# Attention in 64-row halves of TensorE's array: three score banks, untransposed outputs, and the products with the values issued once per two steps of 128 keys

## What is computed

```python
scores = jnp.einsum('bqhd,bkhd->bhqk', q, k) * scale      # 16 heads of 16 features, scale 0.25
probs = jax.nn.softmax(scores, axis=-1)                   # over 1024 keys
out = jnp.einsum('bhqk,bkhd->bqhd', probs, v).reshape(B, S, H)
return out @ wo.T
```

## Time and profile before

| what | us |
|---|---|
| median of 3 runs | 3612.48 |
| the profiled execution | 3616.42 |
| its span | 3614.8 |
| TensorE matmul busy | 3226.5 (89%) |
| TensorE weight load busy | 2116.2 (59%) |
| VectorE busy | 2386.9 (66%) |
| ScalarE busy | 1894.9 (52%) |
| GpSimd busy | 584.8 (16%) |

### The profile page before, as it was taken

The page is one execution under the profiler, slowest core; times in us unless marked ns, Lnnn a source line. Parts: engine busy times, 40 slices in busy tenths (PEclk is TensorE's granted clock), DMA queues, the critical chain, the costliest instruction groups (busy, mean ns, idle before and its releaser), DMA issues. The chain is left out here.

```text
span 3614.8 us, 64942 instructions
## 1 busy us (share of the span) xinstructions
PE 3226.5 (89%) x19056; PEld 2116.2 (59%) x19057; DVE 2386.9 (66%) x4072; ACT 1894.9 (52%) x3374; POOL 584.8 (16%) x846
## 2 busy tenths in 40 slices
PE   5888888849999999999999999997956999999980
PEld 4766666634545455454554545544845888888870
DVE  5666666648888878878878878862567444444436
ACT  3555555513676666666666666664523333333320
POOL 1222222210000000000000000000123444444430
PEclk7899989968999999999999999998878999999995
DMA  1333333321111111111111111114932111111119
GB/s 33 105 104 104 104 104 104 109 99 52 41 54 45 49 51 43 54 41 53 46 48 53 41 54 43 51 31 141 289 105 81 47 51 51 49 49 51 49 46 367
DMA packets 195841, 279.74 MB, mean 77 GB/s; under 512 B 26792, under 2 KB 129472, under 8 KB 195792
## 3 DMA queue, kind: packets, MB, share of 16 engines
q1 hardware_dynamic: 154320, 209.90, 17.9%
q0 software_dynamic: 16128, 44.06, 3.9%
q10 hardware_dynamic: 25344, 25.17, 2.2%
HBM read 158.37 MB, written 118.49 MB: 77 GB/s over the span
## 5 line engine op out<-in xcount | busy, mean ns | idle before, releaser
L779 DVE TENSOR_REDUCE b_mxq<-b_p_m 128x1 f32<-128x1024 f32 x1024 | 1205.5, 1219 | 312.7 <-PE b_p_m L833 304.6
L737 ACT ACTIVATE b_probs<-b_p_e 128x512 f32<-128x512 f32 x2048 | 1112.0, 595 | 509.6 <-PE b_p_e L887 504.8
L887 PE MATMUL b_p_e<-b_qst,b_kst 128*128 128x512 f32 x2048 | 799.7, 436 | 5.9 <-ACT b_probs L737 5.9
L887 PEld LDWEIGHTS b_p_e<-b_qst,b_kst 128*128 128x128 f32 x2048 | 343.5, 187 | 599.6 <-ACT b_probs L737 577.2
L833 PE MATMUL b_p_m<-b_kst,b_qst 128*128 128x512 f32 x2048 | 645.3, 402 | 29.9 <-DMA b_vst<-v_d 24.5
L862 PE MATMUL b_p_o<-b_probs,b_vst 128*32 128x512 f32 x4104 | 546.5, 605 | 0.9 <-ACT b_probs L737 0.9
L833 PEld LDWEIGHTS b_p_m<-b_kst,b_qst 128*128 128x128 f32 x2048 | 388.0, 191 | 116.6 <-issue 24.9
L1443 ACT ACTIVATE d_act<-d_p_up 128x512 f32<-128x512 f32 x136 | 81.3, 597 | 487.3 <-PE d_p_up L1505 487.3
L753 POOL DMA_DIRECT2D o_d<-b_o_s x64 | 34.8, 544 | 1637.9 <-DVE b_o_s L805 1637.9
L1520 PE MATMUL d_p_y<-w2T,d_hT 128*128 x1096 | 258.7, 379 | 0.8 <-ACT d_hT L1437 0.8
L1505 PE MATMUL d_p_up<-up_hi,d_xh 128*128 x544 | 250.7, 461 | 1.5 <-DVE d_xl L1462 1.5
(11 more groups left out here) (259 smaller groups left out, 4160.5 us busy)
## 6 DMA issues: line engine op xcount, KB each, us to landing
b_qst<-qk_d SPq DMA_DIRECT2D x384, 64.0 KB
b_kst<-qk_d SPq DMA_DIRECT2D x384, 64.0 KB
x1y_d<-a_x1y SPq DMA_DIRECT2D x32, 512.0 KB, 3.9
qk_d<-a_hi SPq DMA_DIRECT2D x32, 512.0 KB, 2.8
qk_d<-a_lo SPq DMA_DIRECT2D x32, 512.0 KB, 3.7
v_d<-a_v_s SPq DMA_DIRECT2D x16, 1024.0 KB, 6.9
b_vst<-v_d SPq DMA_DIRECT2D x64, 256.0 KB
c_xy<-x1y_d SPq DMA_DIRECT2D x16, 1024.0 KB
```

What stands on the lines that cost most here:

```text
L737: nc.scalar.activation(probs[e // 2 % 4][:, (e % 2) * 512:(e % 2 + 1) * 512], p_e[e % 2][:], ACT.Exp, scale=SCALE).then_inc(s["e_done"], 1)
L779: V_.reduce_max(mxq[half][:, j:j + 1], p_m[j % 2][:], AX.X).then_inc(s["m_red"], 1)
L887: mm(p_e[a][:], kst[r][h][:, kt * P:(kt + 1) * P], qst[r][:, a * 512:(a + 1) * 512], start=True, stop=True).then_inc(s["e_ps"], 1)
```

## The change

Attention: `kst` has one tile per pair, with head 0 on partitions 0 to 63 and head 1 on 64 to 127, and every score and maximum matmul uses the 64 rows of its head. Queue order on TensorE is now score e, maximum product 4kt + e, for e = 0 to 3, where `column(j)` puts the maximum products of scores of head 0 to head 1 and the other way round. There are three score banks. The values of two steps (16 instructions instead of 8) are issued once per two steps, behind score 2 and maximum product 2 of the even steps. `probs` has eight buffers instead of four. GpSimd splits the maxima before their transpose, which goes into a score bank (slot `NEG_AT + 1`); ScalarE negates. The output is no longer transposed or divided: ScalarE copies `p_o` and GpSimd stores it as it is, denominators included. SyncE issues the loads before the maxima.

Projection: the output is read in transposed form. The denominators are loaded apart (`load_sums`), VectorE takes the reciprocal (`inverses`), ScalarE stores it to DRAM (`store_inverses`), SyncE loads it back broadcast over 16 partitions (`load_inverses`), and GpSimd multiplies (`normalised`). `gather_features`, `transposed` and `output_transposes` are gone.

```diff
@@ softmax_attention @@
-    kst = [[sb(f"kst{r}_{h}", [P, N], f32r) for h in range(2)] for r in range(RING)]
+    kst = [sb(f"kst{r}", [P, N], f32r) for r in range(RING)]
-    probs = [sb(f"probs{r}", [P, N]) for r in range(4)]
+    probs = [sb(f"probs{r}", [P, N]) for r in range(8)]
+    def slot(e):
+        return e if e <= NEG_AT else e + 1          # NEG_AT = 10, EB = 3, SLOTS = 33
+    def column(j):
+        return 1 - j % 2, j // 2
+    def rows(h):
+        return slice(R * h, R * h + R)
...
@@ SyncE @@
-            if more1:
-                maxima(pair + 1, (r + 1) % 2, (r + 1) % RING)
             if more3:
-                sp.wait_ge(s["pv_done"], pair * KT + 2)
+                sp.wait_ge(s["pv_done"], pair * (KT // 2) + 2)
                 load(pair + 3, (r + 3) % RING)
+            if more1:
+                maxima((r + 1) % 2, (r + 1) % RING, pair * SLOTS + (NEG_AT + 5))
@@ ScalarE @@
+        def evacuate(n, half):
+            act.wait_ge(s["pv_done"], n * (KT // 2) + 2)
+            act.wait_ge(s["o_free"], n + 1)
+            nc.scalar.copy(oT[half][:], p_o[:]).then_inc(s["oT_done"], 1)
...
-                if e % 2 == 0:
-                    act.wait_ge(s["pv_done"], pair * KT + (e // 4 + 1))
+                if e % 8 == 0:
+                    act.wait_ge(s["pv_done"], pair * (KT // 2) + (e // 8 + 1))
...
+                if e == 2:
+                    evacuate(pair, r % 2)
@@ GpSimd @@
+        def split(pair, half):
+            pool.wait_ge(s["m_red"], pair * 16 + 18)
+            if not isinstance(pair, int) or pair > 0:
+                pool.wait_ge(s["mT_ps"], pair)
+            pool.sem_inc(s["turn"], 1)
+            g.tensor_copy(hl[:, :, 0], mxq[half][:]).then_inc(s["hi_done"], 1)
+            pool.wait_ge(s["hi_done"], pair + 1)
+            g.tensor_tensor(hl[:, :, 1], mxq[half][:], hl[:, :, 0].bitcast(f32), ALU.subtract).then_inc(s["hl_done"], 1)
         def body(pair, i, r, more1, more, more3):
-            pool.wait_ge(s["o_done"], pair + 3)
-            g.dma_start(o_rows[pair], o_s[r % 2][:].rearrange("p t h e -> p (t h e)")).then_inc(s["o_stored"], 16)
+            pool.wait_ge(s["oT_done"], pair + 2)
+            g.dma_start(o_rows[pair], oT[(r + 1) % 2][:]).then_inc(s["o_stored"], 16)
+            if more:
+                split(pair + 2, r % 2)
@@ TensorE @@
-            h, qt = j // 8, j % 8
+            h, qt = column(j)
             if kh == 0:
                 pe.wait_ge(s["m_red"], pair * 16 + (j + 1))
...
+        def values(r, two, read):
+            pe.wait_ge(s["e_done"], read)
+            for kt in (2 * two, 2 * two + 1):
+                for h in range(2):
+                    for a in range(2):
+                        last = mm(p_o[32 * (2 * h + a):32 * (2 * h + a) + 32, :], vst[r if two >= 0 else (r - 1) % RING][:, kt % KT, h, :],
+                                  probs[(2 * kt + h) % 8][:, a * 512:(a + 1) * 512], start=(kt == 0), stop=(kt == -1))
             last.then_inc(s["pv_done"], 1)
...
+                h, a, u = e // 2, e % 2, slot(4 * kt + e) if more1 else 4 * kt + e
+                pe.wait_ge(s["e_done"], pair * SLOTS + (u + 1))
+                mm(p_e[u % EB][:], kst[r][rows(h), kt * P:(kt + 1) * P], qst[r][rows(h), a * 512:(a + 1) * 512], start=True, stop=True).then_inc(s["e_ps"], 1)
             for kt in range(KT):
+                for e in range(4):
+                    scores(kt, e)
+                    if more:
+                        max_half(pair + 2, r2, 4 * kt + e)
+                    if 4 * kt + e == NEG_AT and more1:
+                        pe.wait_ge(s["e_done"], pair * SLOTS + (NEG_AT + 2))
+                        max_transpose(pair + 1, (NEG_AT + 1) % EB)
+                    if e == 2 and kt % 2 == 0:
+                        if kt == 2:
+                            pe.wait_ge(s["oT_done"], pair + 1)
+                        values(r, kt // 2 - 1, pair * SLOTS + ((slot(4 * kt - 1) if more1 else 4 * kt - 1) + 4))
@@ output_projection_and_gate @@
+        def load_inverses(half, b):                                   # SyncE
+            sp.wait_ge(s[f"rec_st{half}"], b * 16 + 16)
+            sp.sem_inc(s["sp_turn"], 1)
+            for k in range(2):
+                sp.dma_start(rd[half][:, k], rd_d[b, half, 8 * k:8 * k + 8].rearrange("g (o q) -> g o q", o=1).to_broadcast([8, 16, HT])).then_inc(s[f"rd{half}"], 16)
...
+            if after2:
+                sp.wait_ge(s["recip_done"], n + 1)
+                sp.sem_inc(s["sp_turn"], 1)
+                load_sums(half, b + 1)
             if after:
                 if before:
-                    sp.wait_ge(s["orow_done"], n)
-                load_output(n + 1, 1 - half, b_next)
+                    sp.wait_ge(s["oT_done"], n)
+                    sp.sem_inc(s["sp_turn"], 1)
+                load_output(1 - half, b_next)
+                load_inverses(1 - half, b_next)
             sp.wait_ge(s["in_free"], n + 1)
             sp.dma_start(xy[half][:], x1y_v[n]).then_inc(s[f"in{half}"], 16)
...
+        def normalised(n, half, b, before):                           # GpSimd, behind the inverse root of n - 1
+            pool.wait_ge(s[f"oin{half}"], b * 32 + 32)
+            pool.wait_ge(s[f"rd{half}"], b * 32 + 32)
+            if before:
+                pool.wait_ge(s["h_ps"], n - 1)
+            g.tensor_tensor(oT[half][:], oin[half][:], rd[half][:], ALU.mult).then_inc(s["oT_done"], 1)
...
+        def store_inverses(n, half, b):                               # ScalarE, last in its body, for n + 2
+            act.wait_ge(s["recip_done"], n + 1)
+            act.dma_start(rd_d[b, half].rearrange("g (c j) -> (g c) j", c=8), rec[half][:]).then_inc(s[f"rec_st{half}"], 16)
...
             if before:
                 choose(n - 1)
+            if after2:
+                inverses(n + 2, half, b + 1)                          # VectorE
             dve.wait_ge(s["r_done"], n1)
```

More of the change, by code:

```diff
@@ L845, in output_transpose @@
-        def output_transpose(n):
-            pe.wait_ge(s["nm_done"], n + 2 if not isinstance(n, int) else min(n + 2, PAIRS))
-            pe.wait_ge(s["oT_done"], n + 1)
-            pe.wait_ge(s["o_done"], n + 1)
-            for q in range(4):
-                last = tr(p_t[:, q, :], oT[:, q * P:(q + 1) * P], ident[:])
-            last.then_inc(s["oT_ps"], 1)
+            mm(p_m[j % 2][:, kh * 512:(kh + 1) * 512], qst[r][rows(h), qt * P:(qt + 1) * P], kst[r][rows(h), kh * 512:(kh + 1) * 512], start=True, stop=True).then_inc(s["m_ps"], 1)
@@ L869, in _ @@
                 pe.wait_ge(s[f"rows{r}"], 32)
-            for j in range(16):
-                max_scores(pair, pair, j)
+            for half in range(32):
+                max_half(pair, pair, half)
             if pair == 0:
-                max_transpose(0, 0)
+                max_transpose(0, EB - 1)
         for g in range(4):
-            mm(p_o[32 * g:32 * g + 32, :], vst[RING - 1][:, 0, 0, :], probs[2][:, 0:512], start=True, stop=False)
+            mm(p_o[32 * g:32 * g + 32, :], vst[RING - 1][:, 0, 0, :], probs[4][:, 0:512], start=True, stop=False)
         def body(pair, i, r, more1, more, more3):
@@ L1001, in body @@
             g.tensor_tensor(r_s[:], r_s[:], mhalf[:], ALU.pow).then_inc(s["r_done"], 1)
+            if after:
+                normalised(n + 1, 1 - half, b_next, before)
         halves(pool, body)
@@ L1037, in body @@
                 store(n - 1, 1 - half)
-            if after:
-                transposed(n + 1, 1 - half)
             act.wait_ge(s["h_done"], n1)
@@ L1056, in _, with inverses @@
             dve.sem_inc(s[n], c)
+        def inverses(n, half, b):
+            if not isinstance(b, int) or b > 0:
+                dve.wait_ge(s[f"rec_st{half}"], b * 16)
+            dve.wait_ge(s[f"den{half}"], b * 16 + 16)
+            V_.reciprocal(rec[half][:], den_in[half][:]).then_inc(s["recip_done"], 1)
+        for half in (0, 1):
+            inverses(half, half, 0)
         dve.wait_ge(s["wT_ps"], 1)
@@ L1076, in choose, with body @@
             V_.tensor_copy(chosen[:, bass.ds(n * T, T), :], tidx[:, :, 0:2]).then_inc(s["copied"], 1)
-        def body(n, half, b, b_next, before, after):
+        def body(n, half, b, b_next, before, after, after2):
             n1 = n + 1
@@ L1140, in router, with body @@
             i.then_inc(s["lg_ps"], 1)
-        output_transposes(0, 0)
-        def body(n, half, b, b_next, before, after):
+        def body(n, half, b, b_next, before, after, after2):
             n1 = n + 1
```

221 lines of the change are left out of this document (80 added, 141 removed).

## The result

The changed kernel takes 3868.16 us (median of four runs, 3866.1 to 3874.4) where the kernel before takes 3613.43. The ratio is 1.0708, 95% interval 1.0689 to 1.0726: 255 us slower. The forecast was 3716 with a range of 3645 to 3810: the direction was right, 104 us were forecast, and 255 came. The profiled execution took 3867.86 (span 3866.3).

| stretch of the profiled execution | before | after | difference | forecast |
|---|---|---|---|---|
| attention, first to last exponential | 1614.6 | 1743.0 | +128.4 | +21 |
| from there to the first `c_h` | 28.7 | 39.5 | +10.8 | +1 |
| projection, first to last `c_h` | 132.7 | 248.4 | +115.7 | +82 |
| all the rest | 1838.8 | 1835.4 | -3.4 | 0 |

A forecast was written before the change was run, and what follows sets the result against it. Attention was held bound by a chain through two score banks, not TensorE throughput; in projection TensorE and DMA queues were near full. Profiled 3616.42 + 20 attention + 84 projection = 3720, median 3.9 lower: 3716 us, range 3645 to 3810.

The forecast's parts named there:

- Two steps 6.39: Attention: the cycle over one values block takes 6.39 us per two steps, where it was 6.20.
- The idle 1.9 of VectorE: Attention: VectorE has 4.5 us of work in 6.39, so it stands idle 1.9 us per values block.
- the copy on ScalarE costs nothing: Attention: the output copy falls into ScalarE's wait behind the block; uncovered it would cost 0.6 a pair, 37 us.
- the last two pairs: End of attention: pairs without maxima take 5.47 us per two steps against 6.2, -5 us over both.
- a rival with 3%: Attention: TensorE's gaps lower its clock; at half clock block and switches take 1.9 more, about 470 us; 3%.
- the landing of `c_xy`: Projection: the 1 MB load lands in 6.0 us, taken between 5.1 for 512 KB and 9.1 for 1 MB.
- Chain (b): Projection: c_xy's load waits behind the inverses' broadcast; 14.1 us, 14.5 with choice waits, ends last, +82 us.
- The upper end: Projection: +125 us if the 1 MB load lands in 9.1 us.
- Chain (a): Projection: the next half's matmuls wait for the norm and GpSimd's product; 11.4 to 13.1 us a half.
- The start: Before the first c_h: denominators must first go round through DRAM, +2 us; the end of attention loses transposes, -1.
- Without overlap of the halves: Rival, attention: pairs of 64 rows don't overlap beside the blocks; +145 instead of +20, 3841 us; 12%.
- "Faster": Rival, attention: VectorE meets every block with two full banks; two steps 5.06, pair 20.3, -307 us, 3389 in all; 10%.

The follow-up runs named there:

- scores twice: Changed kernel, but every even-numbered score matmul is issued twice into the same bank; 3780.59 us, ratio 1.0466 to the kernel before.
- `c_xy` first: Changed kernel, but SyncE loads c_xy of a half ahead of the broadcast of the next half's inverses; 3824.45 us, ratio 1.0593 to before.
- product first: Changed kernel with `c_xy` first, and GpSimd's product of half n + 1 ahead of the inverse root of half n; 3824.17 us.
- same half: Changed kernel, but each score matmul and the maximum product beside it use the same half of the array's rows; 3905.34 us, ratio 1.0779.
- block later: Changed kernel, but the 16 value instructions stand one matmul pair later, behind m(4kt+3), the output copy behind exponential 3; 3653.68 us, ratio 1.0117.

## Why the prediction was half right

Of the 148 us that the forecast lacks in the profiled execution, the clock in attention is 95, the projection 34, the start 10, and the end of attention with the transpose some 13; the rest of the program gave 3 back.

**Attention at full clock: right.** Two steps 6.39 forecast, 6.38 measured; pair 25.67 forecast, 25.75 with the scores twice. The difference is the transpose of the maxima, 0.21 instead of 0.11, 5 us in all. The idle 1.9 of VectorE is 1.77, s and m start together, and the copy on ScalarE costs nothing. Of the last two pairs, the first takes 5.42 to 5.8 per two steps (forecast 5.47), but the last 7.0 to 7.3, since the clock is low there for 3.4 of every 6.8 us: 8 us more than forecast for the two.

**The clock: this is the step that failed.** In the sum it cost nothing. It was a rival with 3%, priced as half clock throughout (470 us) and put off with "TensorE still streams well over half the time". It came as one stretch of 3.4 us per pair, which costs 27.30 - 25.75 = 1.55 us of the pair and 95 us in all. There were two mistakes: it was treated as all or nothing, and a mean was taken as its measure. The mean doesn't tell these kernels apart: TensorE is 0.89 busy in the changed kernel's windows (1395.9 of 1560) with the clock falling once a pair, and 0.88 (1148.2 of 1300) with the clock at 1.00 when the same values are issued once per step in the same place. The earlier trace rows had shown only that a TensorE busy for 1560 of 1560 us keeps its clock, and the change opened gaps. Why it is exactly one stretch per pair, and at which block, was not settled: in some programs it hits the blocks of kt = 0 and 2 (7.01 and 7.52), in others one of them mostly (7.84 and 6.69), and the sum is 27.30 each time, within 0.02.

**Projection, mechanism right, two terms mis-sized: SyncE's issues and the landing of `c_xy`.** Chain (b), over the inverses and the load of `c_xy`, ended last, as forecast. In the interval shown above, from one `c_h` to the next: 4.38 to the reciprocal (forecast 4.29), 0.55, 1.87 to SyncE's issue (2.4), 1.59 for the issue of the broadcast and the way to the next (0.85), and 8.62 from the issue of `c_xy` to `c_h` (6.0), sum 17.0 against 14.1. The landing was "nearer to the first because this stage now has fewer transfers a microsecond". On average it has; but the broadcast of 512 KB is issued 1.59 us before it on the same queue and probably shares its way (no view gives the landing of `c_xy` alone). The upper end, +125 with a landing of 9.1, was nearly it: +116. Chain (a), over the norm and GpSimd's product, was forecast at 11.4 to 13.1 and is 14.2 with `c_xy` first (means of the 12 middle intervals): 5.6 from `c_h` to the product, where the forecast and the changed kernel itself have 4.98 (ScalarE now begins its squares 1.9 after `c_h` instead of 1.3), 2.34 for the product (2.55), 5.7 for the matmuls (3.70 to 5.39 forecast; up to 6.8 in single halves), and 0.5 in which `c_h` still waited for its load. VectorE's `c_xg` took 3.21 us beside GpSimd's product, 1.14 alone (with product first): not on the path here, and not foreseen.

**The start: +10.8 instead of +1.** The first `c_xy` was issued only at 2624.2, behind both first broadcasts; the denominators' round trip was charged with 2 and the queue behind it with nothing. With `c_xy` first the start is 34.5 instead of 39.5.

**Rivals.** Without overlap of the halves was priced at +145; with the same half it would be (6.61 - 6.38) x 4 x 62 = 57 at most. "Faster" hung on m(4kt+2) starting ahead of the earlier reduction's end. It didn't. But one place further in the queue (block later) VectorE has more in stock at the block, and that run is the fair test of the rival's price: 5.73 per two steps and 23.3 a pair where it says 5.06 and 20.3 (its own terms add up to 0.5 + 3 x 1.13 + 1.22 = 5.1), with VectorE idle for 1.12 per block instead of 0.5.

## What to carry to other kernels

Put a long block of one engine's work where its consumers have the most in stock; here one place in the queue was worth 0.65 us in 6.4, and 0.58 in 3.3. Where a change makes TensorE wait in a stage that was always busy, price the clock as a stretch per period (here 6%), not as a switch, and look at it in short windows; redundant matmuls in its idle time are a quick test. A value that goes round through DRAM is worth a look at what else is in the queues at that moment: the same 32 KB landed after 1.5, 6.6 or 9.2 us.

## What the runs showed of the hardware that was not expected

- The clock fell with TensorE 0.89 busy, and in the records of the 10 us ahead of each fall no idle stretch is longer than 0.39 us (0.31 in the median); with another order it stayed full at 0.88 busy, with idle stretches of up to 0.39 us too and somewhat more idle time in sum (152 us against 137, from 900 to 2200). One difference between the two is that the first has 4.5 us between two blocks with matmuls of 64 rows alone and the second 2.3; that this is the cause was not tried.
- Matmuls of 64 rows on opposite halves start within 10 ns of each other and follow at 0.23 to 0.34 us; with both on the same half two steps take 0.22 us longer.
- The block of 16 value matmuls and the way back to 64-row matmuls take 1.86 us at 2.4 GHz and 2.98 with most of it at 1.2 GHz (blocks of 1203.36 and 1216.75).
- VectorE's four multiplications into `c_xg` take 1.14 us alone and 3.21 beside a GpSimd product of 128x1024, which itself takes 2.34 with or without them.
